# Moving exponentials, weight parts and the half-2 blocks to other slots, and reordering both ends, in a fused attention and router kernel

## What is computed

```python
xn = layernorm(x)
q, k, v = split(silu(xn @ w_qkv.T))                   # 16 heads of 128
out = blockwise_decayed_attention(q, k, v)            # causal, state carried over blocks
out = norm_w * out * rsqrt(mean(out * out) + 1e-6)    # over all 2048 channels
s = (sigmoid(xn @ w_gate.T) * out) @ w_out.T
scores = softmax(xn @ router.T + bias); w, i = top_k(scores, 8)
g = silu(xn * sum(w) + w @ expert_bias[i])
return x + s * g
```

## Time and profile before

| | us |
|---|---|
| median of 3 runs | 1134.75 |
| lowest and highest run | 1131.83, 1135.88 |
| the profiled execution | 1135.64 |
| its span, first to last instruction | 1133.9 |
| TensorE busy | 1101.4 (97%) |
| GpSimd, ScalarE, VectorE busy | 646.7, 630.3, 556.3 |

### The profile page before, as it was taken

The page is one execution under the profiler, slowest core; times in us unless marked ns, Lnnn a source line. Parts: engine busy times, 40 slices in busy tenths (PEclk is TensorE's granted clock), DMA queues, the critical chain, the costliest instruction groups (busy, mean ns, idle before and its releaser), DMA issues.

```text
span 1133.9 us, 15402 instructions
## 1 busy us (share of the span) xinstructions
PE 1101.4 (97%) x6004; PEld 939.7 (83%) x6004; DVE 556.3 (49%) x965; ACT 630.3 (56%) x1118; POOL 646.7 (57%) x634
## 2 busy tenths in 40 slices
PE   7899999999999999999999999999999999999997
PEld 6687878888888888887888888888888888888886
DVE  7244435364555655555444453636354363434436
ACT  6566465465656556555554646556556554655542
POOL 5766456374565646556374875646557375655512
PEclk9899999999999999999999999999999999999999
DMA  3211011131211313232551430111022131111123
GB/s 131 71 38 56 25 51 33 43 112 46 95 66 51 107 45 100 84 97 66 212 188 66 148 103 21 55 38 44 32 81 87 38 112 38 39 37 51 43 75 112
DMA packets 42473, 83.20 MB, mean 73 GB/s; under 512 B 3488, under 2 KB 17952, under 8 KB 42400
## 3 DMA queue, kind: packets, MB, share of 16 engines
q1 hardware_dynamic: 42400, 82.21, 21.9%
HBM read 66.47 MB, written 15.73 MB: 72 GB/s over the span
## 4 chain that ended last, share of the span: by engine, by line
PE 91%; DVE 4%; ACT 3%; issue 1%; POOL 0%; DMA 0%; SPq 0%; DVEq 0%
PE BS L163 8%; PE BS L165 7%; PE BS L164 7%; PE BA L163 5%; PE BA L165 5%; PE BA L164 5%; PE BD L163 5%; PE PO L694 5%; PE BD L165 5%; PE BD L164 5%; PE PX L163 5%; PE PX L165 5%; PE PX L164 5%; PE PS L625 5%; PE PO L679 4%; PE PT L659 4%
## 5 line engine op out<-in xcount | busy, mean ns | idle before, releaser
L473 POOL TENSOR_TENSOR WL<-ST,WH 128x768 fp32r<-128x768 f32 (+1 forms) x128 | 166.3, 1305 | 156.5 <-ACT WH L469 156.4
L473 POOL TENSOR_TENSOR WL<-STG,WH 128x512 fp32r<-128x512 f32 (+1 forms) x128 | 131.1, 1024 | 184.6 <-ACT WH L469 184.6
L163 PE MATMUL BS<-XH,WH 128*128 128x512 f32 x384 | 164.1, 427 | 5.7 <-ACT VT L558 3.8
L165 PE MATMUL BS<-XH,WL 128*128 128x512 f32 x384 | 151.7, 395 | 0.0
L164 PE MATMUL BS<-XL,WH 128*128 128x512 f32 x384 | 150.7, 393 | 0.0
L764 DVE TENSOR_TENSOR Y<-Y,PX 128x512 f32<-128x512 f32 x104 | 71.4, 687 | 131.5 <-PE PX L165 130.7
L743 DVE TENSOR_TENSOR GL<-G,GH 128x512 fp32r<-128x512 f32 x64 | 74.9, 1170 | 96.6 <-ACT GH L739 96.6
L163 PE MATMUL BA<-XH,WH 128*128 128x512 f32 x256 | 109.1, 426 | 5.9 <-ACT VT L593 5.3
L722 POOL TENSOR_TENSOR SS<-SS,SQ 128x512 f32<-128x512 f32 x58 | 89.7, 1546 | 32.3 <-ACT SQ L711 32.3
L163 PE MATMUL BD<-XH,WH 128*128 128x512 f32 x256 | 105.4, 412 | 1.7 <-DVE Q L549 1.7
L534 ACT ACTIVATE BS<-BA 128x512 f32<-128x512 f32 x64 | 37.2, 582 | 122.4 <-PE BA L165 122.4
(11 more groups left out here) (305 smaller groups left out, 2463.1 us busy)
## 6 DMA issues: line engine op xcount, KB each, us to landing
STG<-in_wp SPq DMA_DIRECT2D x80, 512.0 KB, 3.6
XR<-in_x SPq DMA_DIRECT2D x38, 256.0 KB, 4.0
dgd<-XR SPq DMA_DIRECT2D x16, 256.0 KB, 4.3
dxh<-WT SPq DMA_DIRECT2D x8, 448.0 KB, 3.4
dxl<-XR SPq DMA_DIRECT2D x8, 448.0 KB, 4.3
XH<-dxh SPq DMA_DIRECT2D x7, 512.0 KB, 5.1
XL<-dxl SPq DMA_DIRECT2D x7, 512.0 KB, 6.0
XR<-dgd SPq DMA_DIRECT2D x10, 256.0 KB, 4.0
```

The costliest lines, as they stand in the source:

```text
L163: eng.matmul(o, ah, bh, start=first, stop=False, skip_group_check=skip)
L165: return eng.matmul(o, al, bh, start=False, stop=last, skip_group_check=skip)
L473: a = op("pool", lambda e, dst=dst, src=src: e.tensor_tensor(WL[:, u, dst], src, f32(WH[:, u, dst]), ALU.subtract))
```

## The change

The square of the last head goes into SS as all the others do, and `rms_in` sums one part. `ffn_exp` is parted into `ffn_max` (up to the subtraction of the maximum, still slot 29) and `ffn_exp` (the exponential, slot 33); scores, weights and turn go from 31, 33, 35 to 36, 39, 45, the decays from 29 to 33 and their mask from 31 to 36. The half-2 units get other slots, `unit_turn` goes to the head of its slot, and `unit_high` and `unit_low` come one slot later behind it. At the beginning the sums of chunk 0 come ahead of `first_a(0)`, its first two parts and the second norm ahead of `first_a(2)`. Parts 1 to 3 of chunk 1 go from ahead of the loop into slots 2 and 3. At the end `rms_in(0)` comes behind `intra`, and `rms_in(1)` behind batch 0's four last steps and one output half.

```diff
         def squares(c, r, b):
-            late = c == CYC - 1 and r
-            dst = LG if late and b else SQ
-            wait("act", tk["out", c, r, b], tk["lg_read"] if late and b else tk.get("sq_read"))
-            q = op("act", lambda e: e.activation(dst[:, :], PO[:, :], ACT.Square))
+            wait("act", tk["out", c, r, b], tk.get("sq_read"))
+            q = op("act", lambda e: e.activation(SQ[:, :], PO[:, :], ACT.Square))
             tk["po"] = (q,)
-            if late:
-                tk["sq", b] = q
-                return
             wait("pool", q)
...
-        def ffn_exp(b):
+        def ffn_max(b):
             wait("pe", tk["lg"], *tk.get("px", ()))
...
-            a = op("dve", lambda e: e.tensor_tensor(L, SC[:, :, :], mx[:, :].unsqueeze(2).to_broadcast([128, 4, NE]),
-                                                    ALU.subtract))
-            wait("act", a)
+            tk["lx"] = op("dve", lambda e: e.tensor_tensor(
+                L, SC[:, :, :], mx[:, :].unsqueeze(2).to_broadcast([128, 4, NE]), ALU.subtract))
+
+        def ffn_exp(b):
+            wait("act", tk["lx"])
             tk["le"] = op("act", lambda e: e.activation(L, L, ACT.Exp))
...
-        def rms_in(b, bank, at_, free, more=None):
-
+        def rms_in(b, bank, at_, free):
             wait("pe", tk["ss", b], *free)
-            if more is not None:
-                wait("pe", tk["sq", b])
-            parts = [SS[:, b, :]] + ([] if more is None else [more[:, :]])
...
-                for s, f, *a in ((27, ffn_logits, h, b), (29, ffn_exp, b), (31, ffn_scores, b), (33, ffn_weights, b),
-                                 (35, ffn_turn, b)):
+                for s, f, *a in ((27, ffn_logits, h, b), (29, ffn_max, b), (33, ffn_exp, b), (36, ffn_scores, b),
+                                 (39, ffn_weights, b), (45, ffn_turn, b)):
...
-                    plan(base + 29, decays, lo, hi)
-                    plan(base + 31, decays_masked, lo, hi)
+                    plan(base + 33, decays, lo, hi)
+                    plan(base + 36, decays_masked, lo, hi)
...
-        for t, (load, stats, norm, s0, s1) in enumerate(((121, 124, 126, 131, 145), (147, 150, 153, 159, 173),
-                                                         (174, 176, 178, 181, 189), (190, 192, 194, 201, 207))):
+        for t, (load, stats, norm, s0, s1) in enumerate(((119, 122, 125, 129, 143), (144, 147, 149, 153, 161),
+                                                         (162, 168, 169, 171, 179), (180, 182, 184, 187, 199))):
...
-                for i, f in enumerate((unit_turn, unit_mix, unit_more, unit_high, unit_low)):
+                at.setdefault(s, []).insert(0, (unit_turn, (t, kk)))
+                for i, f in ((1, unit_mix), (2, unit_more), (4, unit_high), (5, unit_low)):
                     plan(s + i, f, t, kk)
...
         first_stats(1, (0, 1), t1)
+        w_sums(0)
         first_a(0, PS, d0[0])
         first_a(1, PT, d0[1])
-        w_parts(0, (0,))
         first_norm1((0, 1), t1)
         first_stats(1, (2, 3), t1)
+        w_parts(0, (0, 1))
+        first_norm1((2, 3), t1)
         first_a(2, PO, d0[2])
         first_a(3, PX, d0[3])
-        w_sums(0)
-        first_norm1((2, 3), t1)
...
         first_mix(0, *pairs[0])
-        w_parts(0, (1,))
         first_mix(1, *pairs[1])
...
         w_sums(1)
-        w_parts(1, (1, 2, 3))
+        plan(2, w_parts, 1, (1,))
+        at[3].insert(0, (w_parts, (1, (2, 3))))
...
         gate_low(c, 1, 0)
-        rms_in(0, PT, 0, tk["pt"], SQ)
         halves(0, 0, (0, 1))
         intra(c, 1, 1)
+        rms_in(0, PT, 0, tk["pt"])
         halves(0, 0, (2, 3))
...
         halves(1, 0, range(4))
-        rms_in(1, PT, 16, (tk["rr", 0],), LG)
         finals(0, "pool")
         seed(1, 3, PX, tk["y_read", 0, 0])
         finals(1, "dve")
-        halves(0, 1, range(4))
         finals(2, "pool")
         finals(3, "dve")
+        halves(0, 1, (0,))
+        rms_in(1, PT, 16, (tk["rr", 0],))
+        halves(0, 1, (1, 2, 3))
         halves(1, 1, range(4))
```

More of the change, by code:

```diff
@@ L867, in rms @@
             tk["px"] = (rms_in(b, PX, 0, tk.get("px", ())),)
-        def rms_in(b, bank, at_, free, more=None):
+        def rms_in(b, bank, at_, free):
             wait("pe", tk["ss", b], *free)
-            if more is not None:
-                wait("pe", tk["sq", b])
-            parts = [SS[:, b, :]] + ([] if more is None else [more[:, :]])
             def pe(e):
                 for t in range(4):
-                    for i, a in enumerate(parts):
-                        m = e.matmul(bank[:, at_ + t * 4:at_ + (t + 1) * 4], a[:, t * 128:(t + 1) * 128], ones[:, :],
-                                     start=(i == 0), stop=(i + 1 == len(parts)))
+                    m = e.matmul(bank[:, at_ + t * 4:at_ + (t + 1) * 4], SS[:, b, t * 128:(t + 1) * 128], ones[:, :],
+                                 start=True, stop=True)
                 return m
```

## The result

The changed kernel takes **1118.39 us** (median of 5 runs, 1117.01 to 1119.55) against 1134.75 before: ratio 0.9859, 95% interval 0.9840 to 0.9877, so 16.4 us less. The forecast was 1119.5. The profiled execution took 1118.39 with a span of 1116.6, 17.25 less than the span before.

A forecast was written before the change was run, and what follows sets the result against it. TensorE, busy 97% of the span, was taken as the bound, so only its waits or slow-clock stretches could go. Terms: 2.0 - 5.8 - 4.8 - 0.4 - 5.3 - 1.6 = -15.9 us; forecast 1119.5, range 1112 to 1127.

The forecast's parts named there:

- Beginning: New order ahead of the first product: nb held up by GpSimd's subtraction, first product 0.3 to 2.7 us later; +2.0 us.
- Chunk 1's parts: Parts 1 to 3 into slots 2 and 3: 3.78 us wait and 2.4 of half clock go, 0.4 stays; -5.8 us.
- Exponentials, first half: Two blocks, slot 29 to 33: of about 7.6 us of waits and half clock, 2.8 stays; -4.8 us.
- Second half's exponentials: Same move without the six long exponentials: two waits of some 0.2 us vanish; -0.4 us.
- Half-2 blocks: New slots for the half-2 units remove 6.3 us of TensorE waits, 1.0 kept for VectorE-GpSimd collisions; -5.3 us.
- The end: VectorE bounds the last tiles; batch 0's four first start the chain up to 3.2 us earlier; -1.6 us net.
- Only move their wait: Rival, first-half exponentials: TensorE waits 3 to 4 us at (5, 7), clock falls, term 0: 1124.5 us; chance 0.15.
- Beginning eats the gap: Rival: some 3 us idle before first_blocks(2) brings slow clock, up to 3 us more: 1123.5 us; chance 0.10.
- Slower: Rival: U's store is late, so unit_turn's copy, ScalarE and the next ypart wait: 1137 us or more; chance 0.02.
- Everything pays: Rival: no wait left at the exponentials or in the blocks, nb in first: 1113 us; chance 0.07.

The follow-up runs named there:

- slot 43: Changed kernel with exponentials and decays moved to slot 43, scores and mask to 45, weights to 47, turn to 51: 1115.70 us, ratio 0.9827.

## Why the prediction was right

**The sum.** The terms as added give 1134.75 - 15.9 = 1118.85 for the median; the 1119.5 that I wrote does not follow from them. Two smaller slips change nothing: the loop has 448 slots (16 times 28) and not 452, and the earlier start of `first_blocks(2)` is 21.1 by its own rows and not 20.9.

**Beginning, +2.0:** right in size by luck, wrong in its make-up. The chain to `first_blocks(2)` was right: `nb` 1.22 us long, and 22.01 (forecast 22.1). But the copies and mixes behind it caught up more than I allowed: at full clock the new order costs 1.0 (18.5 against 17.5). The other 1.05 is the clock, which I had kept in a rival at 0.10. That rival's mechanism came, and with it the sign by which I said that I would be wrong (over 3 us idle before 26, and the clock falls there); its price, "up to 3 us more", was too high: `first_blocks(2)` and `(3)` at half clock delayed (0, 1) by 1.05 to 1.1 in three traces and 2.2 in one. So two errors of about 1 us, the clock left out and the delay of copies and mixes taken too long, cancelled. And the part is a loss, as forecast: with the old order the kernel took 1116.03.

The rule of the Trainium skill ("SBUF — State Buffer", section Who interferes with whom) agrees: the port that VectorE shares with GpSimd is an exclusive lock, and `nb` took 1.22 us beside the subtraction and 0.16 ahead of it.

**Chunk 1's parts, -5.8:** 5.8 at (0, 4), alone as in company, and (0, 4) waits 0.4 for L542, as forecast. The 0.3 that comes back by (1, 7) was not foreseen; net 5.5.

**Exponentials, first half, -4.8:** 5.0 in this pair of traces, 4.2 against the second trace of before, where block 1 kept its clock. The 1.4 us that I said would stay per block was 1.42 and 1.44 (slot 43 against slot 33), 1.0 of it shown as the wait at `inter`, and none at (5, 7). What failed is the tacit step that such a wait always brings half clock: where it does not, the term is 1.0 for a block, not 2.5. So part of the gain hangs on what the clock does in the kernel before.

The drain that the Trainium skill ("ScalarE: Activation LUTs", What ACT_TABLE_LOAD costs) puts behind a load is not in these rows: Exp starts 0.02 us behind its load (96.08 + 1.28, then 97.38).

**Second half's exponentials, -0.4:** 0.9 between the two traces, 0.6 when put back alone (2.1 at (32, 6), 2.7 at (48, 6)), 0.3 between the second traces of both kernels (270.45 and 270.15 us from (32, 6) to (48, 6), where the first have 270.72 and 269.79). Two executions of one kernel differ here by as much as the term, so its size is not settled.

**Half-2 blocks, -5.3:** 6.0, but not as summed. 1.5 of 6.3 us of waits is left (0.9 of it behind L549, at 425.85), half a microsecond more than the 1.0 that I kept for collisions, so the waits gave 4.8; and 1.2 more came off than any wait shows, which no term had.

**The end, -1.6:** 1.9 (1.7 in the median when undone). The timeline of VectorE, against the earlier trace rows, and two rows of GpSimd's show both sides of the sum:

```profile
1098.35 0.16 DVE L878 TENSOR_SCALAR sv<-PT 128x4 f32<-128x4 f32 x1 [1.90 <-PE PT L871]
...
1101.02 1.37 DVE L738 TENSOR_TENSOR GL<-G,GH 128x512 fp32r<-128x512 f32 x1 [0.46 <-ACT GH L734]
1102.31 0.74 DVE L934 SCALAR_TENSOR_TENSOR XR<-PX,rr,XR 128x512 f32<-128x512 f32 x1
...
1108.80 0.75 DVE L934 SCALAR_TENSOR_TENSOR STG<-BS,rr,STG 128x512 f32<-128x512 f32 x1 [1.19 <-issue]
```

```profile
1100.54 1.30 POOL L717 TENSOR_TENSOR SS<-SS,SQ 128x512 f32<-128x512 f32 x1 [0.50 <-ACT SQ L709]
...
1107.68 1.02 POOL L880 TENSOR_TENSOR rr<-sv,half_ 128x4 f32<-128x4 f32 x1 [0.70 <-DVE sv L878]
```

The 3.2 us ahead of the tiles are gone. The last `gate_low` (1101.02) takes 1.37 us instead of the 0.69 of before, beside GpSimd's addition into SS, which started at 1100.54, and VectorE stands 1.19 us ahead of 1108.80 while GpSimd makes batch 1's power: both as listed.

**The rivals.** "Only move their wait" fell: 1.0 us at `inter`, none at (5, 7), clock full. "Beginning eats the gap" came in its mechanism but not in its price, as said above. "Slower" fell: no unit copy (L970) waited for a store. "Everything pays" fell too, with waits left in the beginning and at `inter`; a time that low took other edits (1111.6). The sum of the traces, 2.1 - 5.8 + 0.3 - 5.0 - 6.0 - 0.9 - 1.9 = -17.2, was 1.3 more than forecast, mostly half-2 blocks and second-half exponentials. The medians lie 16.4 apart, 0.5 more than the sum; the execution traced before took 0.9 longer than its median.

## What to carry to other kernels

Ask of a long piece on a helper engine not how long it is but what stands behind it, and put it where the next thing behind it is needed latest (and, for a table switch, where a switch comes anyway). Compute a wait without and with the slow clock behind it and keep both as bounds, since the same wait may be paid once or twice. A tiny instruction at the head of a chain deserves its own place: hold the neighbour on the other engine for it, not the other way round.

## What the runs showed of the hardware

The same idle time of TensorE, 2.40 us in the same place, was followed by the 0.50 clock in one kernel and by 1.00 in another, and two executions of the kernel before differed in it behind waits of 2.63 and 2.52 us at 169; the price of the fall was 1.4 to 1.6 us per block. Behind 1.96 us the clock fell in one trace, behind 3.34 and 3.46 us it stayed in two.

A VectorE instruction on 128x2 numbers took 1.22 us when a GpSimd subtraction had started 0.06 us ahead of it, and 0.16 us when that subtraction was held back. A table load of ScalarE took 1.28 us, and the function behind it started 0.02 us after its end.
